# Fourth layer: one 2048-column transposition for a pair of heads instead of two of 1024 columns

## The reference

```python
q, k, v = (x @ Wq + bq), (x @ Wk + bk), (x @ Wv + bv)     # split into 8 heads of 64
scores = einsum('bmhd,bnhd->bhmn', q, k) / 8 + edge_bias[edges]
scores = leaky_relu(scores, 0.2)
attn = softmax(where(edges > 0, scores, -1e9), axis=-1)
out = einsum('bhmn,bnhd->bmhd', attn, v).reshape(b, m, h * d)
x = layernorm(x + (out @ Wp + bp))
```

## Time and profile before

| | |
|---|---|
| median of three runs | 5111.82 us (5109.01 to 5113.97) |
| profiled execution | 5109.67 us, its span 5107.9 us |
| fourth layer in that span | from about 3720 us to the end |
| busy share of the span | DVE 95%, ACT 93%, PE 90%, POOL 75% |
| L854 transposes, by output and source | 342 + 170, mean 1225 ns |

### The profile page before, as it was taken

One profiled execution on the slowest core, in us unless ns is written; L12 is line 12 of the kernel. 1 busy time (PEld: TensorE's weight loads), 2 busy tenths in 40 slices (PEclk: granted clock), 3 DMA queues, 4 the chain that ended last, 5 costly groups with the idle time before them and its releaser, 6 DMA issues. The chain is left out here.

```text
span 5107.9 us, 118848 instructions
## 1 busy us (share of the span) xinstructions
PE 4593.3 (90%) x48920; PEld 1811.6 (35%) x48920; DVE 4832.7 (95%) x5683; ACT 4760.1 (93%) x5793; POOL 3822.1 (75%) x3482
## 2 busy tenths in 40 slices
PE   7888888888888999999999999997889999999998
PEld 2222222222222222232332323224445555555554
DVE  7999999999999999999999999996779999999998
ACT  7999999999999999999999999996779999999997
POOL 8999999999999999999999999993303223322333
PEclk9999999999999999999999999997879999999999
DMA  1000000010000000000000000004410111010100
GB/s 53 32 31 27 32 32 32 26 32 32 26 32 32 18 11 9 12 11 11 10 11 12 12 9 12 11 9 137 137 26 16 24 24 24 16 24 24 25 16 13
DMA packets 154143, 138.54 MB, mean 27 GB/s; under 512 B 53318, under 2 KB 120646, under 8 KB 153606
## 3 DMA queue, kind: packets, MB, share of 16 engines
q1 hardware_dynamic: 152902, 130.87, 8.8%
q10 hardware_dynamic: 704, 0.07, 0.0%
HBM read 103.64 MB, written 18.87 MB: 24 GB/s over the span
## 5 line engine op out<-in xcount | busy, mean ns | idle before, releaser
L200 POOL TENSOR_SCALAR a_hid_p<-a_BLOS,a_PHI,a_PLO 128x1024 f32<-128x1024 f32 x2720 | 3188.6, 1192 | 97.3 <-PE apsS L330 90.5
L459 DVE SCALAR_TENSOR_TENSOR a_hid_p<-apsB,a_THI,a_hid_p 128x1024 f32<-128x1024 f32 x2560 | 3075.6, 1278 | 16.3 <-POOL a_hid_p L200 14.4
L330 PE MATMUL apsS<-a_hid_p,a_sel_high 128*32 128x512 f32 x10880 | 2633.5, 597 | 169.9 <-ACT a_hid_a L367 97.5
L330 PE MATMUL apsS<-a_hid_a,a_sel_high 128*32 128x512 f32 x6144 | 1912.8, 596 | 47.0 <-ACT a_hid_a L367 25.1
L330 PE MATMUL apsS<-a_hid_a,a_sel_low 128*32 128x512 f32 x5504 | 1680.0, 596 | 109.0 <-ACT a_hid_a L367 58.4
L367 ACT ACTIVATE a_hid_a<-a_BHI,a_ALH 128x1024 f32<-128x1024 f32 x1536 | 1687.7, 1143 | 0.0
L367 ACT ACTIVATE a_hid_a<-a_BLO,a_ALH 128x1024 f32<-128x1024 f32 x1376 | 1531.1, 1142 | 0.0
L330 PEld LDWEIGHTS apsS<-a_hid_p,a_sel_high 128*32 128x32 f32 x10880 | 587.6, 109 | 938.8 <-issue 534.9
L761 PE MATMUL m3S<-xT,Q 64*128 64x512 f32 x2048 | 594.3, 654 | 28.1 <-ACT x_even L805 14.3
L330 PEld LDWEIGHTS apsS<-a_hid_a,a_sel_high 128*32 128x32 f32 x6144 | 419.7, 109 | 559.9 <-issue 301.2
L330 PEld LDWEIGHTS apsS<-a_hid_a,a_sel_low 128*32 128x32 f32 x5504 | 374.5, 109 | 647.4 <-issue 323.9
(11 more groups left out here) (184 smaller groups left out, 3910.2 us busy)
## 6 DMA issues: line engine op xcount, KB each, us to landing
a_adj_in<-adj SPq DMA_DIRECT2D x64, 512.0 KB, 3.7
adj_in<-adj SPq DMA_DIRECT2D x64, 512.0 KB, 4.7
mask_rows<-a_mask SPq DMA_DIRECT2D x64, 256.0 KB, 2.2
a_mask<-mask_rows SPq DMA_DIRECT2D x64, 256.0 KB, 2.6
mask<-mask_rows SPq DMA_DIRECT2D x64, 256.0 KB, 2.8
Xr<-x_odd SPq DMA_DIRECT2D x128, 64.0 KB, 2.1
out<-yn SPq DMA_DIRECT2D x64, 32.0 KB, 1.5
x_even<-x SPq DMA_DIRECT2D x1, 256.0 KB, 3.0
```

Source lines behind the costliest of these rows:

```text
L200: gp.tensor_scalar(hid_p[:, at % RING_P, :], BLOS[:, g % 2, :], PHI[:, g % 2, m:m + 1], PLO[:, g % 2, m:m + 1], ALU.min, ALU.max).then_inc ...
L330: last = pe.matmul(psS[32 * q:32 * q + 32, h * HALF:(h + 1) * HALF], sel[:, 28 - 4 * p:60 - 4 * p], unit, start=s == 0 and layer == 0, sto ...
L459: dve.scalar_tensor_tensor(out=hid_p[:, at % RING_P, :], in0=psB[:, :], scalar=THI[:, g % 2, m:m + 1], in1=hid_p[:, at % RING_P, :], op0=A ...
```

## The change

The three slots' buffers become one tensor of 2048 columns each, head 0 first and head 1 behind it. VectorE's two transpositions of a slot become one: its input is read as head, key block, 32 columns, and its output pattern goes head, key block, 32 columns through `ZT`, so each head's blocks land where they did. It waits for both exponentials of the slot, and it is issued behind the minima of the next slot, where the second of the two was. `turned` now counts slots instead of heads, and the waits of TensorE and ScalarE follow.

```diff
-    Z = lambda k, e: Zs[2 * (k % 3) + e]
+    Z = lambda k, e: Zs[k % 3][:, e * n:(e + 1) * n]
...
-                    pe.wait_ge(turned, HEADS * (m + 1))
+                    pe.wait_ge(turned, PAIRS * (m + 1))
...
-                    act.wait_ge(turned, 2 * (k - 3) + e + 1)
+                    act.wait_ge(turned, k - 2)
...
-            def turn(k, e):
+            def turn(k):
                 m, h = divmod(k, PAIRS)
-                dve.wait_ge(probs_ready, 2 * k + e + 1)
-                if h == 0 and e == 0 and m >= 3:
+                dve.wait_ge(probs_ready, 2 * k + 2)
+                if h == 0 and m >= 3:
                     dve.wait_ge(weighed, m - 2)
-                at = 32 * (2 * h + e)
-                dve.transpose(ZT[:, m % 3, :, at:at + 32], Z(k, e).rearrange("p (b i) -> p b i", i=32)).then_inc(turned, 1)
+                dve.transpose(ZT[:, m % 3, :, 64 * h:64 * h + 64].rearrange("p b (e i) -> p e b i", e=2),
+                              Zs[k % 3].rearrange("p (e b i) -> p e b i", e=2, i=32)).then_inc(turned, 1)
...
-                if 1 <= i <= U:
-                    turn(i - 1, 0)
                 for job in aux_jobs(i, 0):
                     aux(job)
                 if i < U:
                     masked_min(i, 0)
                     masked_min(i, 1)
                 if 1 <= i <= U:
-                    turn(i - 1, 1)
+                    turn(i - 1)
...
-            more = sg("Z3", [P, 2, n])
+            more = sg("Z3", [P, 2 * n])
...
-                       Z=[X[0][:, i * n:(i + 1) * n] for i in range(4)] + [more[:, i, :] for i in range(2)],
+                       Z=[X[0][:, 0:2 * n], X[0][:, 2 * n:4 * n], more[:, :]],
```

## The result

The changed kernel took 5122.37 us (median of 14 runs, 5117.90 to 5128.41), the kernel before 5109.94 (14 runs, 5107.30 to 5113.97): a ratio of 1.0025, 95% interval 1.0017 to 1.0032, so 12 us slower. The prediction's number was 5116, +4.

A forecast was written before the change was run, and what follows sets the result against it. VectorE's queue sets the pace now; after the change a loop through TensorE and ScalarE does. Ordinary tiles +3.5, x-turning tiles -0.4, first tile +1, tail +0.1: +4 on 5111.82 gives 5116 us, range 5100 to 5137.

The forecast's parts named there:

- the loop: Last turn through TensorE and ScalarE to third slot's minima: 6.19 us against VectorE's 5.84, so VectorE waits 0.35 a tile.
- The queue: VectorE's own instructions: the merged transposition takes 2.22 us instead of 2.29 for two, saving 0.07.
- The rival with 2.11: Merged turn takes 2.11 us, three in the loop, ordinary tile 20.30, total 5096; shares chance 0.20 with VectorE's queue alone.
- the one with 2.29 or more: Longer transposition costs 2.29 to 2.36 us, saving nothing or losing: 5129 to 5141; chance 0.15.
- The stretch from there to the next turn: VectorE from third slot's minima to the tile's last turn: 14.44 us, making an ordinary tile 20.63, 0.09 more.
- The first tile: Fourth layer's first tile: last turn ends one transposition later against the minima, up to 1.16 us, taken as 1.
- hidden by 0.16: Crossing after Q in an ordinary tile: minimum can start at 15.99 us, VectorE arrives at 16.15, so no wait.
- The wait for Q: TensorE's idle time before the next tile's scores, forecast to rise from 0.28 to about 0.6 us.
- Tiles that turn x: Tiles also turning the next batch's x: another VectorE wait of 0.37 us, ending at 21.62, 0.03 less than now.
- Row-term tiles: Seven tiles making the row term: old waits for ScalarE go, new ones come, within 0.1 us, counted as 0.
- second rival: GpSimd's addition goes before a minimum more than 0.16 us late, costing some 0.4 a tile: 5140; chance 0.15.
- The first rival: Saving felt: VectorE's queue alone counts, 0.28 us off each tile, 5095, or merged turn 2.11, 5096; chance 0.20.

The follow-up runs named there:

- e6: Changed kernel with GpSimd's additions made to wait until the second slot's minima are done: 5121.79 us, 1.0027 of the kernel before.
- e12: Changed kernel with Q and statistics ahead of the merged turn, GpSimd's additions later, one weighing step instead of three in the first gap: 5056.85 us.
- e3: Changed kernel with the next tile's Q added ahead of the merged turn instead of behind it: 5110.17 us, 1.0004 of the kernel before.
- e1: Kernel before with its two transpositions kept separate, both behind the next slot's minima (new order without merging): 5125.60 us, ratio 1.0034.
- e2: Changed kernel with the two statistics operations moved ahead of the merged turn: 5116.98 us, 1.0015 of the kernel before.
- e5: Kernel before with GpSimd's additions made to wait until the second slot's minima are done: 5085.67 us, ratio 0.9953.
- e11: Kernel before with GpSimd's additions later and the next tile's Q ahead of the second turn: 5074.14 us, ratio 0.9934.

## Why the prediction was right in its mechanism, and which term was too small

The direction, the loop and the wait came out as forecast; the size did not, +12 us against +4. An ordinary tile lost 0.31 us where 0.09 was forecast. That the measured time lies well inside 5100 to 5137 owes much to the width that the rivals gave this range.

- **The queue.** "2.22 us for the merged operation": 2.23. The rival with 2.11 is out, and so is the one with 2.29 or more.
- **The loop.** "Sum 6.19": 6.19 in every kernel that has the full loop in the new order, with the 0.35 us of VectorE's wait that followed from it. e6 shows that it bounds, e12 that VectorE's wait goes when it is cut.
- **The stretch from there to the next turn** was put at 14.44, and was 14.66 (4426.86 to 4441.52). This is the mis-sized term: 20.85 instead of 20.63. 0.14 of it is the step from statistics to a minimum, 0.52 where I took the 0.38 that the earlier trace rows show from statistics to a transposition. The other 0.08 is spread: the two pairs of minima that no longer stand behind a transposition take 2.28 and 2.30 instead of 2.26, the three turns 6.69 instead of 6.66, Q 0.57 instead of 0.58. I moved operations past each other and kept the start-to-start times of the old neighbours. 39 x 0.22 = 8.6 us is about the whole difference between +4 and +12.
- **Terms that happened to cancel.** The first tile was given +1 and cost nothing: from the first copy of x to the first reciprocal both kernels take 88.4 us. Three ordinary tiles took 21.21, because the first minimum behind the statistics waited 0.41 for ScalarE, a crossing that the prediction had "hidden by 0.16": +1.
- **The wait for Q** came out at 0.54 us, "about 0.6" in the prediction. But the 0.28 that it is compared with was not shown as a wait for Q: the earlier trace rows have it released by ScalarE's leaky step.
- **Tiles that turn x**: 21.62 forecast, 21.65 measured; e3 shows that the wait in them was for Q. **Row-term tiles**: 0 forecast, 22.30 and 23.92 against 22.31 and 23.89.
- **GpSimd.** The order product, minimum, minimum stayed, and so did its price: the second minimum lasts 1.74 (1.75 before). GpSimd never got in front. In the tiles behind one that turns x or makes the row term that minimum came 0.15 to 0.16 late, just under the "more than 0.16" of the second rival, so its case did not arise, if only by a little. The variance operation does meet a minimum now and lasts 1.17 instead of 0.19; the minima beside it take 1.15 each, as others behind a wait do, so no price for VectorE can be seen.
- **The first rival**, VectorE's queue alone, would have brought 20.26. Even without the wait the queue would be, by an estimate from the timeline, 20.85 - 0.35 - 0.04 = 20.46, only 0.08 under the old one: the new neighbours ate most of the saving. That would be 5 us in all.
- My chance for slower by over 0.2% was 0.31, and that for the likeliest case, no change, 0.52. The measured +0.25% lies just over that line, and the side was the less likely one of my table.

Not tried: how the 0.24 us between aggregation and minimum come about, whether from the operation or from its wait.

## What to carry to other kernels

Where the busiest engine shows no idle time, measure the slack of every loop that passes through it before reordering its queue: here 0.84 us stood between a free edit and a loss, and a 1.1 us move used it up. When the order changes, the times between starts change too; take each from a row with the new neighbours, or bound it. And test a suspected bound with one edit in both kernels, one that shortens the queue alone: 23 us in one and nothing in the other says more than any timeline.

## What the runs showed of the hardware that I had not expected

- The fixed part of a transposition is nearly all overlapped: 1024 columns last 1.20 to 1.24 us and take 1.12 to 1.16 from start to start, 2048 columns last 2.30 and take 2.23. The Trainium skill (VectorE: DVE Perf Modes, fixed extra latency of SBUF-source operations) gives about 150 cycles, 0.156 us, for each instruction. The durations agree: from 1.225 to 2.305 us (means) the second 1024 columns add 1.08, which leaves 0.145 as fixed. The times from start to start do not: the merging saved 0.06.
- A minimum that reads two SBUF tensors costs VectorE 0.53 us when GpSimd's 256-column addition (0.72 alone) lands between it and its neighbour. Moving that addition beside a transposition brought 23 us in the old order, twice what the studied change cost.
- The tile that makes the row term takes 22.3 us at a granted clock of 1.00 over the tile and 23.9 at 0.93, 1.6 us each, and three in e6 took 25.6 at 0.87. In the profiles of the kernel before, the changed one, e1, e2, e5 and e6, 26 of 42 such tiles are at the lower clock; with Q made earlier (e3, e11, e12) none of 21 is, though e3 has three other tiles at 0.92 to 0.93. In the kernel before TensorE stands idle for 0.79 us until Q is added, in tiles of both clocks; in e11 it does not wait there. There is one profile of each kernel, so how much of this is the kernel and how much the execution is not shown.
